# The last tile of targets walked in two passes of two row blocks each

## The chip, the cores and the metric

The kernel runs on one core of a Trainium2 chip. The metric is the device time of one execution in microseconds (us). Three runs of the kernel before took 810.81, 811.78 and 812.55 us; the median is 811.78 us. The profile is that of one more execution, which took 810.83 us.

## The reference, cut to what matters

Two graph layers over 4096 nodes with 128 features and a 4096 x 4096 integer adjacency matrix. The first takes, for each node, the maximum of its neighbours' features; the second is a graph attention layer. Only the second is touched by the change:

```python
h = jnp.maximum(_layernorm(x, axis=-1), 0.0)
x = x + _L0_gnn_ref(h, adj)                    # masked maximum over the neighbours
h = jnp.maximum(_layernorm(x, axis=-1), 0.0)
# _L1_gnn_ref(h, adj, W, a):
h = input @ W
e = (h @ a1)[:, None] + (h @ a2)[None, :]
e = jnp.where(e > 0, e, ALPHA * e)
e = jnp.where(adj > 0, e, NEG)
attention = jax.nn.softmax(e, axis=1)
h_prime = attention @ h
x = x + jax.nn.elu(h_prime)
```

## The kernel before, in words

The first 520 us or so make the masked maximum and also write the transposed adjacency, as 16-bit numbers, to `edge_units` in the chip's memory. The attention layer starts near 536 us. Its targets (the rows of the result) are cut into `TILES` = 8 tiles of `TI` = 512 targets, each of `ROWS` = 4 row blocks of 128. For each tile the kernel walks over `C` = 32 chunks of 128 sources. One pair (tile q, chunk c) is a step, and the list `ORDER` (line 166) gives the order of the steps: tiles 0 and 1 are walked in alternation, tiles 2 to 7 one after another, 32 steps each.

One step is this. VectorE (DVE) makes the unnormalised attention weights of 128 sources by 512 targets with a single instruction, `weigh(n)` (line 1016): the maximum of a row (`limit`) and a per-partition scalar (`slope`), times the adjacency. TensorE (PE) then does `mix(n)` (line 674): one float32 product for each of the four row blocks, with the weights loaded into the array and `wh` (128 features and a column of ones, so 129 columns) streamed past. Each float32 product is two records of the profile, so a step is eight. The sums of a tile stay in two PSUM banks (`out_ps`); even and odd tiles use different ones.

The two engines are tied by counting semaphores. `made` counts the weights that VectorE has made, `mixed` the steps that TensorE has done. There are `WEIGHTS` = 6 weight buffers, so VectorE may start step n only when step n-6 is done (line 1015). The adjacency comes in units of 8 steps of 1 MB each, four a tile, into `EDGES` = 4 buffers. SyncE (SP) loads a unit as soon as the last step that reads the unit before it in that buffer is made (line 289).

When a tile's last step is done, its output goes through these functions:

- `invert(q)` (line 1019) on VectorE copies the four columns of sums from PSUM (line 1023) and takes their reciprocal (line 1025). It stands in VectorE's program behind the weight of the fifth step of the next tile.
- `norm(q)` on ScalarE (ACT) scales the four row blocks from PSUM into `att` (line 477), and later takes an exponential (line 482).
- `cut(q)` on GpSimd (POOL), for tiles 0 to 6: two tensor-scalar instructions (lines 353 and 354), two tensor-tensor additions (lines 356 and 359), all 128 x 512, and the store (line 361).
- For tile 7, the last, the same arithmetic stands on VectorE (lines 1183 to 1189), behind four small instructions that test the size of the denominators (lines 1175 to 1179), and SyncE stores (line 293).

Behind that, a flag (`den_flag`, line 1191) is read by TensorE, ScalarE, VectorE and SyncE, which then branch over a part of the program that isn't run for these inputs. With that the kernel ends.

Of the kernel before, what the change touches and what calls it, by code (L numbers as in the profile page):

```python
# [79 lines left out]
def layers(nc, adj, x_rows, w, a, edge_units, subset_max, out_rows, w_sb, a12, w_in, hs, x1_in, h_hi, h_lo, ident_h, ident32, order_w, bit_w, word,  # L80
# [4 lines left out]
    with ctx:  # L85
# [80 lines left out]
        ORDER = [(q, c) for lo, hi in PARTS for q in range(2) for c in range(lo * ROWS, hi * ROWS)]  # L166
        ORDER += [(q, c) for q in range(2, TILES) for c in range(C)]
        PLACE = {at: n for n, at in enumerate(ORDER)}
        ENDS = [PLACE[q, C - 1] for q in range(TILES)]
        LOADED = list(dict.fromkeys(q * UNITS + c // (UNIT * PAIR) for q, c in ORDER))  # L170
# [4 lines left out]
        EDGES = 4  # L175
        WEIGHTS = 6
        ALL = TILES * C
# [59 lines left out]
        with nc.Block() as block:  # L237
            @block.sync
            def _(sp):
# [52 lines left out]
                sp.wait_ge(last_done, 1)  # L292
                sp.dma_start(out_rows[:, q * ROWS:(q + 1) * ROWS, :], low[:, q % 2, :, :]).then_inc(last_stored, 16)
                sp.wait_ge(last_stored, 16)
                sp.wait_ge(stored[0], 16 * (TILES // 2))
                sp.wait_ge(stored[1], 16 * (TILES // 2 - 1))

# [12 lines left out]
            def _(pool):  # L310
# [36 lines left out]

                def cut(q):
                    if q >= 2:
                        pool.wait_ge(stored[q % 2], 16 * (q // 2))  # L350
                    pool.wait_ge(normed, (q + 1) * ROWS)
                    al, ll = att[:, q % 2, :, :], low[:, q % 2, :, :]
                    nc.gpsimd.tensor_scalar(ll, al, 0.0, None, ALU.min).then_inc(low_made, 1)  # L353
                    nc.gpsimd.tensor_scalar(al, al, 0.0, -1.0, ALU.max, ALU.add).then_inc(kept_made, 1)
                    pool.wait_ge(kept_made, q + 1)
                    nc.gpsimd.tensor_tensor(al, al, x1[:, q * ROWS:(q + 1) * ROWS, :], ALU.add).then_inc(summed_up, 1)
                    pool.wait_ge(summed_up, q + 1)
                    pool.wait_ge(low_exp, q + 1)
                    nc.gpsimd.tensor_tensor(ll, ll, al, ALU.add).then_inc(finished, 1)
                    pool.wait_ge(finished, q + 1)  # L360
                    nc.gpsimd.dma_start(out_rows[:, q * ROWS:(q + 1) * ROWS, :], ll).then_inc(stored[q % 2], 16)

                for q in range(TILES - 1):
                    cut(q)

            @block.scalar
            def _(act):
# [102 lines left out]

                def norm(q):
                    act.wait_ge(rden_made, q + 1)
                    if q >= 2:
                        act.wait_ge(finished, q - 1)
                    for b in range(ROWS):
                        r = q * ROWS + b
                        nc.scalar.activation(att[:, q % 2, b, :], out_ps(q, b)[:, 0:D], ACT.Copy, scale=rden[:, r:r + 1]).then_inc(normed, 1)  # L477
                    if q == TILES - 1:
                        act.wait_ge(last_low, 1)
                    else:  # L480
                        act.wait_ge(low_made, q + 1)
                    nc.scalar.activation(low[:, q % 2, :, :], low[:, q % 2, :, :], ACT.Exp).then_inc(low_exp, 1)

# [34 lines left out]
                for q in range(2, TILES):  # L518
                    if q + 1 < TILES:
                        bound(q + 1)  # L520
                    norm(q)

                act.wait_ge(flag_made, 1)
# [14 lines left out]
            def _(pe):  # L538
# [122 lines left out]
                def mix(n):  # L661
                    q, c = ORDER[n]
                    pe.wait_ge(made, n + 1)
                    if q == 0:
                        pe.wait_ge(wh_made, c + 1)
                        if c % ROWS == 0:
                            pe.wait_ge(wh_last, c // ROWS + 1)
                    if c == 0:
                        if q == 1:
                            pe.wait_ge(joined, 6)  # L670
                        elif q >= 2:
                            pe.wait_ge(normed, (q - 1) * ROWS)
                    for b in range(ROWS):
                        last = nc.tensor.matmul(out_ps(q, b), weight[:, n % WEIGHTS, b * P:(b + 1) * P], wh[:, c, :],  # L674
                                                start=c == 0 and b % 2 == 0, stop=c == C - 1 and b % 2 == 1)
                    last.then_inc(mixed, 1)
# [140 lines left out]
            def _(dve):  # L817
# [201 lines left out]
                def invert(q):  # L1019
                    dve.wait_ge(mixed, ENDS[q] + 1)  # L1020
                    for b in range(ROWS):
                        r = q * ROWS + b
                        V.tensor_copy(den[:, r:r + 1], out_ps(q, b)[:, D:D + 1]).then_inc(den_made, 1)
                    dve.wait_ge(den_made, (q + 1) * ROWS)
                    V.reciprocal(rden[:, q * ROWS:(q + 1) * ROWS], den[:, q * ROWS:(q + 1) * ROWS]).then_inc(rden_made, 1)  # L1025

# [102 lines left out]
                for n in range(ALL):  # L1129
                    q, c = ORDER[n]  # L1130
                    if c == 0:
                        cap(q)
# [39 lines left out]
                al, ll = att[:, q % 2, :, :], low[:, q % 2, :, :]  # L1172
                dve.wait_ge(rden_made, TILES)
                dve.wait_ge(curves, GR)
# [10 lines left out]
                dve.wait_ge(last_sum, 1)  # L1185
                V.tensor_tensor(al, al, x1[:, q * ROWS:(q + 1) * ROWS, :], ALU.add).then_inc(last_sum, 1)
                dve.wait_ge(last_sum, 2)
                dve.wait_ge(low_exp, TILES)
                V.tensor_tensor(ll, ll, al, ALU.add).then_inc(last_done, 1)
# [61 lines left out]
```

## Time and profile before

| | |
|---|---|
| runs, lowest / median / highest | 810.81 / 811.78 / 812.55 us |
| profiled execution: time | 810.83 us |
| its span, first to last instruction | 809.0 us |
| TensorE busy | 709.9 us (88%) |
| VectorE busy | 720.6 us (89%) |
| ScalarE busy | 485.5 us (60%) |
| GpSimd busy | 282.8 us (35%) |

The time lies 1.9 us above the span: that is what lies around the instructions. "Busy" is the time in which an engine has an instruction in hand, and the records of neighbouring instructions may overlap, so the distance from one start to the next says more than a duration. All times in the rows are counted from the start of the span. The granted clock is the share of full speed (2.4 GHz) that TensorE was given.

### The profile page before, as it was taken

The page shows a single profiled execution, that of the slowest core. Times are in us where ns is not written, and L with a number is a line of the kernel's source. Part 1 is how long each engine was busy: PE and PEld are TensorE (multiplying, and loading weights), DVE is VectorE, ACT ScalarE, POOL GpSimd, SP SyncE. Part 2 cuts the span into 40 slices and gives each one's busy share as a digit, 9 for nine tenths or more (in the row PEclk, how much of TensorE's full clock was granted, in tenths as well). Part 3 has the DMA queues.
Part 4 walks back from the last instruction along what each step waited for, and adds up shares of the span by engine and source line. Part 5 has one row for each costly group of instructions (what it writes and reads, how often), then busy time and mean ns, then how long its engine had stood idle before and what let it go on. Part 6 is the DMA issues. An engine that isn't in the chain of part 4 may idle for free.

```text
span 809.0 us, 14805 instructions
## 1 busy us (share of the span) xinstructions
PE 709.9 (88%) x5594; PEld 488.4 (60%) x5594; DVE 720.6 (89%) x1116; ACT 485.5 (60%) x614; POOL 282.8 (35%) x258
## 2 busy tenths in 40 slices
PE   1788999999999999999999999476889999999995
PEld 1344444444444444444444445355889999999995
DVE  8899889999999999999999999886678998898994
ACT  2978888888888888888888886235423010010000
POOL 0611034434434435434444345354202531232130
PEclk9999999999999999999999999699899999999998
DMA  9799767997777867877787744523313544444410
GB/s 307 248 369 358 255 228 256 261 296 254 244 220 243 260 223 225 260 237 218 248 254 223 232 152 133 181 48 121 119 53 156 184 140 142 163 156 164 131 60 15
DMA packets 62857, 162.55 MB, mean 201 GB/s; under 512 B 6400, under 2 KB 11136, under 8 KB 58688
## 3 DMA queue, kind: packets, MB, share of 16 engines
q1 hardware_dynamic: 53776, 138.75, 49.5%
q0 software_dynamic: 9008, 22.82, 11.4%
q8 instruction: 47, 0.77, 0.4%
q14 instruction: 26, 0.21, 0.1%
HBM read 117.51 MB, written 44.04 MB: 200 GB/s over the span
## 4 chain that ended last, share of the span: by engine, by line
PE 45%; ACT 23%; DVE 17%; issue 11%; DMA 2%; POOL 1%; ACTq 0%; DVEq 0%; SPq 0%
PE pick_ps L674 27%; ACT edge_t L373 10%; DVE acc L850 7%; ACT depth L382 6%; PE order_ps L559 6%; PE pick_ps L578 6%; ACT first L381 4%; DVE rest L839 2%; PE late_ps L591 2%; PE late_ps L550 2%; DMA subset_max<-keys 1%; DVE rest L1016 1%; PE late_ps L658 1%; PE order_ps L643 1%; DVE acc L978 1%
## 5 line engine op out<-in xcount | busy, mean ns | idle before, releaser
L850 DVE TENSOR_TENSOR acc<-pick_ps,acc 128x1024 f32<-128x1024 f32 x248 | 302.9, 1221 | 27.9 <-PE pick_ps L578 23.7
L345 POOL DMA_INDIRECT found<-subset_max,entry x192 | 205.2, 1069 | 288.7 <-DVE entry L862 180.7
L674 PE MATMUL pick_ps<-keys,rest 128*128 128x129 f32 x2048 | 240.4, 279 | 13.3 <-DVE rest L1016 12.6
L674 PEld LDWEIGHTS pick_ps<-keys,rest 128*128 128x128 f32 x2048 | 236.6, 195 | 19.6 <-DVE rest L1016 17.6
L1016 DVE SCALAR_TENSOR_TENSOR rest<-depth,acc,stage 128x512 f32<-128x512 f32 x256 | 200.2, 812 | 28.2 <-PE pick_ps L674 9.4
L381 ACT ACTIVATE first<-order_ps,neg 128x1024 f16<-128x1024 f32 x128 | 142.5, 1113 | 61.3 <-PE order_ps L559 61.3
L382 ACT ACTIVATE depth<-order_ps,mid 128x1024 f16<-128x1024 f32 x128 | 141.6, 1107 | 0.0
L373 ACT ACTIVATE edge_t<-late_ps 128x1024 f16<-128x1024 uint16 x128 | 131.0, 1023 | 2.8 <-PE late_ps L550 2.8
L559 PE MATMUL order_ps<-edge_t,order_w 128*128 128x512 f16 x256 | 79.2, 392 | 36.9 <-ACT edge_t L373 29.7
L578 PE MATMUL pick_ps<-first,h_hi 128*128 128x512 f16 x256 | 97.6, 381 | 6.8 <-DVE acc L850 6.7
L550 PEld LDWEIGHTS late_ps<-ident_h,stage 128*128 128x128 f16 x1024 | 69.3, 99 | 48.8 <-DMA stage<-adj 13.1
L578 PE MATMUL pick_ps<-second,h_hi 128*128 128x512 f16 x256 | 97.4, 380 | 0.4 <-DVE acc L850 0.4
L578 PE MATMUL pick_ps<-first,h_lo 128*128 128x512 f16 x256 | 97.6, 381 | 0.0
L578 PE MATMUL pick_ps<-second,h_lo 128*128 128x512 f16 x256 | 97.2, 380 | 0.0
L550 PE MATMUL late_ps<-ident_h,stage 128*128 128x128 f16 x1024 | 80.3, 223 | 17.1 <-DMA stage<-adj 13.1
L477 ACT ACTIVATE keys<-pick_ps,acc 128x128 f32<-128x128 f32 x32 | 9.1, 368 | 129.4 <-DVE acc L1025 129.4
L591 PEld LDWEIGHTS late_ps<-bit_w,rest 128*128 128x128 f16 x1024 | 62.6, 98 | 29.4 <-issue 14.5
L591 PE MATMUL late_ps<-bit_w,rest 128*128 128x128 f16 x1024 | 78.6, 220 | 0.0
L559 PEld LDWEIGHTS order_ps<-edge_t,order_w 128*128 128x128 f16 x256 | 15.5, 98 | 97.0 <-ACT edge_t L373 91.1
L353 POOL TENSOR_SCALAR keys<-keys 128x512 f32<-128x512 f32 x7 | 13.1, 1878 | 148.0 <-ACT keys L477 148.0
L833 DVE TENSOR_SCALAR second<-depth 128x2048 f16<-128x2048 f16 x64 | 44.4, 693 | 0.0
L839 DVE TENSOR_SCALAR rest<-depth 128x2048 f16<-128x2048 f16 x64 | 43.8, 685 | 0.0
(140 smaller groups left out, 519.3 us busy)
## 6 DMA issues: line engine op xcount, KB each, us to landing
stage<-adj SPq DMA_DIRECT2D x64, 1024.0 KB, 5.4
edge_units<-edge_t SPq DMA_DIRECT2D x64, 512.0 KB, 4.4
stage<-edge_units SPq DMA_DIRECT2D x32, 1024.0 KB, 4.9
subset_max<-keys POOLq DMA_DIRECT2D x12, 512.0 KB, 8.7
found<-subset_max,entry POOLq DMA_INDIRECT x192, 4.3
best<-x SPq DMA_DIRECT2D x4, 512.0 KB, 6.1
subset_max<-x POOLq DMA_DIRECT2D x4, 512.0 KB, 8.9
out<-keys POOLq DMA_DIRECT2D x7, 256.0 KB, 2.8
```

Of the source, the lines that this page charges most:

```text
L345: nc.gpsimd.indirect_dma_start(found[:, n % NG, s, :], None, subset_max, bass.IndirectOffsetOnAxis(entry[:, n, s:s + 1], 0)).then_inc(gath ...
L373: nc.scalar.activation(edge_t[:, g % (KEPT * KEEP), :], flip_ps[:, :].bitcast(U16), ACT.Sign).then_inc(edge_ready, 1)
L381: nc.scalar.activation(first[:, g % 4, :], order_ps[:, :], ACT.Relu, scale=-1.0, bias=neg[:, :]).then_inc(first_ready, 1)
L382: nc.scalar.activation(depth[:, g % 4, :], order_ps[:, :], ACT.Abs, bias=mid[:, :]).then_inc(depth_ready, 1)
L550: last = nc.tensor.transpose(flip_ps[:, c * TI + r * P:c * TI + (r + 1) * P], low[:, (s * PAIR + c) * P:(s * PAIR + c + 1) * P], ident_h[: ...
L559: last = nc.tensor.matmul(order_ps[:, c * TI:(c + 1) * TI], order_w[:, :], edge_t[:, g % (KEPT * KEEP), c * TI:(c + 1) * TI], start=True, ...
L578: last = nc.tensor.matmul(pick_ps[k][:, c * TI:(c + 1) * TI], half_h[:, p * PAIR + c, :], s[:, c * TI:(c + 1) * TI], start=part == 0, stop ...
L591: last = nc.tensor.matmul(key_ps[:, r * P:(r + 1) * P], rest[:, g % RESTS, c * TI + r * P:c * TI + (r + 1) * P], bit_w[:, b, :], start=Fal ...
L674: last = nc.tensor.matmul(out_ps(q, b), weight[:, n % WEIGHTS, b * P:(b + 1) * P], wh[:, c, :], start=c == 0 and b % 2 == 0, stop=c == C - ...
L839: V.tensor_scalar(rest[:, to:to + 2, :], depth[:, at:at + 2, :], MID - 1.5, None, ALU.is_lt).then_inc(rest_ready, 1)
L850: V.tensor_tensor(acc[:, q % 2, :], pick_ps[k][:, :], acc[:, q % 2, :], ALU.max).then_inc(raised, 1)
L1016: V.scalar_tensor_tensor(out=weight[:, n % WEIGHTS, :], in0=limit[:, q % 2, :], scalar=slope[:, c:c + 1], in1=units[:, m % EDGES, k * TI:( ...
```

## The change

`ORDER` gets 32 further steps: tile 7 is now walked twice. `SEGS` lists nine segments (tile, first row block, last row block): tiles 0 to 6 whole, then row blocks 0 and 1 of tile 7, then row blocks 2 and 3. `span_of(n)` gives the row blocks of step n. In a step of the two last segments VectorE makes 256 columns of weights and TensorE does two products. `ENDS` has nine entries, one for each segment, and `invert`, `norm` and `cut` count segments instead of tiles. The first half of tile 7 now goes through GpSimd's `cut`, 256 columns wide, and GpSimd's store; VectorE's closing arithmetic and SyncE's store take only the second half. The units of adjacency are still loaded once each (`LOADED` drops repetitions), and all four units of tile 7 have a buffer of their own.

```diff
-        PLACE = {at: n for n, at in enumerate(ORDER)}
-        ENDS = [PLACE[q, C - 1] for q in range(TILES)]
+        ORDER += [(TILES - 1, c) for c in range(C)]
+        SEGS = [(q, 0, ROWS) for q in range(TILES - 1)] + [(TILES - 1, 0, ROWS // 2), (TILES - 1, ROWS // 2, ROWS)]
+        ENDS = [n for n, (q, c) in enumerate(ORDER) if c == C - 1]
+        span_of = lambda n: (0, ROWS) if n <= ENDS[TILES - 2] else SEGS[TILES - 1][1:] if n <= ENDS[TILES - 1] else SEGS[TILES][1:]
...
-                sp.dma_start(out_rows[:, q * ROWS:(q + 1) * ROWS, :], low[:, q % 2, :, :]).then_inc(last_stored, 16)
+                sp.dma_start(out_rows[:, q * ROWS + ROWS // 2:(q + 1) * ROWS, :], low[:, q % 2, ROWS // 2:ROWS, :]).then_inc(last_stored, 16)
...
-                for q in range(TILES - 1):
-                    cut(q)
+                for k in range(len(SEGS) - 1):
+                    cut(k)
...
-                    for b in range(ROWS):
+                    for b in range(lo, hi):
                         r = q * ROWS + b
                         nc.scalar.activation(att[:, q % 2, b, :], out_ps(q, b)[:, 0:D], ACT.Copy, scale=rden[:, r:r + 1]).then_inc(normed, 1)
...
-                    for b in range(ROWS):
+                    for b in range(*span_of(n)):
                         last = nc.tensor.matmul(out_ps(q, b), weight[:, n % WEIGHTS, b * P:(b + 1) * P], wh[:, c, :],
...
-                    V.scalar_tensor_tensor(out=weight[:, n % WEIGHTS, :], in0=limit[:, q % 2, :], scalar=slope[:, c:c + 1],
-                                           in1=units[:, m % EDGES, k * TI:(k + 1) * TI], op0=ALU.max, op1=ALU.mult).then_inc(made, 1)
+                    lo, hi = (b * P for b in span_of(n))
+                    V.scalar_tensor_tensor(out=weight[:, n % WEIGHTS, lo:hi], in0=limit[:, q % 2, lo:hi], scalar=slope[:, c:c + 1],
+                                           in1=units[:, m % EDGES, k * TI + lo:k * TI + hi], op0=ALU.max, op1=ALU.mult).then_inc(made, 1)
...
-                invert(TILES - 1)
+                invert(TILES)
...
-                al, ll = att[:, q % 2, :, :], low[:, q % 2, :, :]
-                dve.wait_ge(rden_made, TILES)
+                al, ll = att[:, q % 2, ROWS // 2:ROWS, :], low[:, q % 2, ROWS // 2:ROWS, :]
+                dve.wait_ge(rden_made, TILES + 1)
```

On VectorE, from the sixth step of tile 7 to the closing arithmetic (`rest` is the memory that the weights lie in, `acc` holds the sums and their reciprocals), before:

```order
L1023 COPY acc<-pick_ps 128x1 [waits mixed]
L1023 COPY acc<-pick_ps 128x1 x3
L1025 RECIPROCAL acc<-acc 128x4 [waits den_made]
L1016 SCALAR_TENSOR_TENSOR rest<-depth,acc,stage 128x512 [waits mixed] x3
L1016 SCALAR_TENSOR_TENSOR rest<-depth,acc,stage 128x512 [waits mixed,edge_in1]
L1016 SCALAR_TENSOR_TENSOR rest<-depth,acc,stage 128x512 [waits mixed] x7
L1016 SCALAR_TENSOR_TENSOR rest<-depth,acc,stage 128x512 [waits mixed,edge_in2]
L1016 SCALAR_TENSOR_TENSOR rest<-depth,acc,stage 128x512 [waits mixed] x7
L1016 SCALAR_TENSOR_TENSOR rest<-depth,acc,stage 128x512 [waits mixed,edge_in3]
L1016 SCALAR_TENSOR_TENSOR rest<-depth,acc,stage 128x512 [waits mixed] x7
L1023 COPY acc<-pick_ps 128x1 [waits mixed]
```

The end of the first pass and the start of the second on the same engine, after (line 1022 is `weigh`, lines 1030 and 1032 are `invert`):

```order
L1022 SCALAR_TENSOR_TENSOR rest<-depth,acc,stage 128x256 [waits mixed,edge_in3]
L1022 SCALAR_TENSOR_TENSOR rest<-depth,acc,stage 128x256 [waits mixed] x7
L1022 SCALAR_TENSOR_TENSOR rest<-depth,acc,stage 128x256 [waits mixed,edge_in0]
L1022 SCALAR_TENSOR_TENSOR rest<-depth,acc,stage 128x256 [waits mixed] x4
L1030 COPY acc<-pick_ps 128x1 [waits mixed]
L1030 COPY acc<-pick_ps 128x1
L1032 RECIPROCAL acc<-acc 128x2 [waits den_made]
L1022 SCALAR_TENSOR_TENSOR rest<-depth,acc,stage 128x256 [waits mixed] x3
L1022 SCALAR_TENSOR_TENSOR rest<-depth,acc,stage 128x256 [waits mixed,edge_in1]
```

Where 32 instructions of 512 columns stood for tile 7, there are now 64 of 256 columns, with a second pair of copies and a reciprocal between the passes, and the waits on `mixed` and on the units occur twice.

On GpSimd, the end of the program before:

```order
L353 TENSOR_SCALAR keys<-keys 128x512 [waits normed,stored0]
L354 TENSOR_SCALAR keys<-keys 128x512
L356 TENSOR_TENSOR keys<-keys,x 128x512 [waits kept_made]
L359 TENSOR_TENSOR keys<-keys 128x512 [waits low_exp,summed_up]
L361 DMA out<-keys 128x4x128 [waits finished]
```

And after (lines 356 to 364 are what 353 to 361 were):

```order
L364 DMA out<-keys 128x4x128 [waits finished]
L356 TENSOR_SCALAR keys<-keys 128x256 [waits normed,stored1]
L357 TENSOR_SCALAR keys<-keys 128x256
L359 TENSOR_TENSOR keys<-keys,x 128x256 [waits kept_made]
L362 TENSOR_TENSOR keys<-keys 128x256 [waits low_exp,summed_up]
L364 DMA out<-keys 128x2x128 [waits finished]
```

GpSimd has one more round, of half the width, behind that of tile 6.

## Rows read from the trace of the kernel before

**Rows 1.** The page: span, and busy time of each engine (section 1).

```profile
span 809.0 us, 14805 instructions
PE 709.9 (88%) x5594; PEld 488.4 (60%) x5594; DVE 720.6 (89%) x1116; ACT 485.5 (60%) x614; POOL 282.8 (35%) x258
```

**Rows 2.** Chain that ended last, tiles 6 and 7: start us, us, what.

```profile
721.37 28.59 PE pick_ps L674 x256
749.95 0.86 PE order_ps L643 x2
750.81 49.15 PE pick_ps L674 x440
```

**Rows 3.** Same chain, its last piece, behind the last product.

```profile
799.98 0.37 DVE acc L1023 x4
800.35 0.02 issue
800.37 0.19 DVE acc L1025
800.56 0.02 issue
800.59 1.15 ACT keys L477 x4
801.74 0.03 issue
801.76 0.05 DVEq L1182
801.81 0.05 issue
801.86 0.43 DVE keys L1183
802.29 0.35 DVE keys L1184
...
802.66 0.70 DVE keys L1186
...
803.38 0.69 DVE keys L1189
804.08 0.06 DVE den_flag L1191
```

**Rows 4.** Timeline around the start of tile 7: start us, us, instruction.

```profile
771.40 0.36 DVE L1023 COPY acc<-pick_ps 128x1 f32<-128x1 f32 x4
771.79 0.18 DVE L1025 RECIPROCAL acc<-acc 128x4 f32<-128x4 f32 x1
771.88 2.06 DVE L1016 SCALAR_TENSOR_TENSOR rest<-depth,acc,stage 128x512 f32<-128x512 f32 x3
772.00 1.14 ACT L477 ACTIVATE keys<-pick_ps,acc 128x128 f32<-128x128 f32 x4 [20.40 <-DVE acc L1025]
773.30 1.98 POOL L353 TENSOR_SCALAR keys<-keys 128x512 f32<-128x512 f32 x1 [21.10 <-ACT keys L477]
774.15 14.08 DVE L1016 SCALAR_TENSOR_TENSOR rest<-depth,acc,stage 128x512 f32<-128x512 f32 x16 [0.21 <-PE pick_ps L674]
775.26 2.25 POOL L354 TENSOR_SCALAR keys<-keys 128x512 f32<-128x512 f32 x1
777.59 1.27 POOL L356 TENSOR_TENSOR keys<-keys,x 128x512 f32<-128x512 f32 x1
778.94 1.59 POOL L359 TENSOR_TENSOR keys<-keys 128x512 f32<-128x512 f32 x1
```

**Rows 5.** Timeline of VectorE alone, short stretches of tile 7.

```profile
774.15 2.59 DVE L1016 SCALAR_TENSOR_TENSOR rest<-depth,acc,stage 128x512 f32<-128x512 f32 x3 [0.21 <-PE pick_ps L674]
...
777.65 1.76 DVE L1016 SCALAR_TENSOR_TENSOR rest<-depth,acc,stage 128x512 f32<-128x512 f32 x1
779.33 2.41 DVE L1016 SCALAR_TENSOR_TENSOR rest<-depth,acc,stage 128x512 f32<-128x512 f32 x2
783.65 0.74 DVE L1016 SCALAR_TENSOR_TENSOR rest<-depth,acc,stage 128x512 f32<-128x512 f32 x1
784.32 1.40 DVE L1016 SCALAR_TENSOR_TENSOR rest<-depth,acc,stage 128x512 f32<-128x512 f32 x2
```

**Rows 6.** The same engine in tile 2, working off a backlog, and GpSimd beside it.

```profile
629.99 2.56 DVE L1016 SCALAR_TENSOR_TENSOR rest<-depth,acc,stage 128x512 f32<-128x512 f32 x2
631.01 2.56 DVE L1016 SCALAR_TENSOR_TENSOR rest<-depth,acc,stage 128x512 f32<-128x512 f32 x2
632.47 1.76 DVE L1016 SCALAR_TENSOR_TENSOR rest<-depth,acc,stage 128x512 f32<-128x512 f32 x2
630.71 1.73 POOL L353 TENSOR_SCALAR keys<-keys 128x512 f32<-128x512 f32 x1
632.42 1.92 POOL L354 TENSOR_SCALAR keys<-keys 128x512 f32<-128x512 f32 x1
```

**Rows 7.** VectorE's instructions by form, whole span: busy us, mean ns of one.

```profile
L873 DVE TENSOR_TENSOR found<-found 128x384 f32<-128x384 f32 x32 | 17.6, 551 | 1.3 <-issue 1.3
L873 DVE TENSOR_TENSOR found<-found 128x128 f32<-128x128 f32 x32 | 9.1, 283 | 0.2
L1023 DVE COPY acc<-pick_ps 128x1 f32<-128x1 f32 x32 | 2.8, 150 | 5.3 <-PE pick_ps L674 4.6
```

**Rows 8.** TensorE's line 674 from 771.4 to 785.7: ns min/median/max.

```profile
L674 PE MATMUL pick_ps<-keys,rest x130: 273/276/276, 771.2 to 785.6; 128*128 128x129 f32 x130
```

**Rows 9.** Windows: PE, PEld, DVE, ACT, POOL busy, granted clock, DMA share, GB/s.

```profile
563.04:566.45 3.41, 0.72 (x6) 0.72 (x7) 2.55 (x9) 2.04 (x6) 1.80 (x2) 1.00 0.21 37
563.00:575.00 12.00, 9.27 (x68) 9.27 (x69) 10.75 (x22) 5.40 (x14) 6.63 (x6) 0.86 0.36 106
597.17:600.59 3.42, 2.14 (x20) 1.95 (x19) 2.33 (x5) 0.00 (x0) 0.00 (x0) 1.00 0.00 0
600.59:604.00 3.41, 2.48 (x21) 2.28 (x21) 3.19 (x13) 0.30 (x1) 0.00 (x0) 1.00 0.02 5
771.40:800.00 28.60, 28.55 (x256) 28.35 (x254) 22.00 (x33) 1.77 (x5) 7.89 (x5) 1.00 0.04 11
```

**Rows 10.** DMA issues of the whole run (page, section 6) and the last store's.

```profile
stage<-edge_units SPq DMA_DIRECT2D x32, 1024.0 KB, 4.9
...
out<-keys SPq DMA_DIRECT2D x1, 256.0 KB, 2.4
```

More of the change, by code:

```diff
@@ L176, in layers @@
         WEIGHTS = 6
-        ALL = TILES * C
+        ALL = len(ORDER)
         PER = UNIT * PAIR
@@ L292, in _ @@
                 sp.wait_ge(last_done, 1)
-                sp.dma_start(out_rows[:, q * ROWS:(q + 1) * ROWS, :], low[:, q % 2, :, :]).then_inc(last_stored, 16)
+                sp.dma_start(out_rows[:, q * ROWS + ROWS // 2:(q + 1) * ROWS, :], low[:, q % 2, ROWS // 2:ROWS, :]).then_inc(last_stored, 16)
                 sp.wait_ge(last_stored, 16)
                 sp.wait_ge(stored[0], 16 * (TILES // 2))
-                sp.wait_ge(stored[1], 16 * (TILES // 2 - 1))
+                sp.wait_ge(stored[1], 16 * (TILES // 2))
                 sp.wait_ge(flag_made, 1)
@@ L346, in _, with cut @@
                                                      bass.IndirectOffsetOnAxis(entry[:, n, s:s + 1], 0)).then_inc(gathered[n % NG][s % 2], 16)
-                def cut(q):
+                def cut(k):
+                    q, lo, hi = SEGS[k]
                     if q >= 2:
                         pool.wait_ge(stored[q % 2], 16 * (q // 2))
-                    pool.wait_ge(normed, (q + 1) * ROWS)
-                    al, ll = att[:, q % 2, :, :], low[:, q % 2, :, :]
+                    pool.wait_ge(normed, q * ROWS + hi)
+                    al, ll = att[:, q % 2, lo:hi, :], low[:, q % 2, lo:hi, :]
                     nc.gpsimd.tensor_scalar(ll, al, 0.0, None, ALU.min).then_inc(low_made, 1)
                     nc.gpsimd.tensor_scalar(al, al, 0.0, -1.0, ALU.max, ALU.add).then_inc(kept_made, 1)
[L355 to L358, printed above, removed]
+                    pool.wait_ge(kept_made, k + 1)
+                    nc.gpsimd.tensor_tensor(al, al, x1[:, q * ROWS + lo:q * ROWS + hi, :], ALU.add).then_inc(summed_up, 1)
+                    pool.wait_ge(summed_up, k + 1)
+                    pool.wait_ge(low_exp, k + 1)
                     nc.gpsimd.tensor_tensor(ll, ll, al, ALU.add).then_inc(finished, 1)
-                    pool.wait_ge(finished, q + 1)
-                    nc.gpsimd.dma_start(out_rows[:, q * ROWS:(q + 1) * ROWS, :], ll).then_inc(stored[q % 2], 16)
-                for q in range(TILES - 1):
-                    cut(q)
+                    pool.wait_ge(finished, k + 1)
+                    nc.gpsimd.dma_start(out_rows[:, q * ROWS + lo:q * ROWS + hi, :], ll).then_inc(stored[q % 2], 16)
+                for k in range(len(SEGS) - 1):
+                    cut(k)
             @block.scalar
@@ L469, in gather_wh, with norm @@
                         nc.scalar.activation(wh[:, c, 0:D], wh_of(g, c % ROWS), ACT.Copy, scale=gain[:, c:c + 1]).then_inc(wh_made, 1)
-                def norm(q):
-                    act.wait_ge(rden_made, q + 1)
+                def norm(k):
+                    q, lo, hi = SEGS[k]
+                    act.wait_ge(rden_made, k + 1)
                     if q >= 2:
                         act.wait_ge(finished, q - 1)
-                    for b in range(ROWS):
+                    for b in range(lo, hi):
                         r = q * ROWS + b
                         nc.scalar.activation(att[:, q % 2, b, :], out_ps(q, b)[:, 0:D], ACT.Copy, scale=rden[:, r:r + 1]).then_inc(normed, 1)
-                    if q == TILES - 1:
+                    if k == TILES:
                         act.wait_ge(last_low, 1)
                     else:
-                        act.wait_ge(low_made, q + 1)
-                    nc.scalar.activation(low[:, q % 2, :, :], low[:, q % 2, :, :], ACT.Exp).then_inc(low_exp, 1)
+                        act.wait_ge(low_made, k + 1)
+                    nc.scalar.activation(low[:, q % 2, lo:hi, :], low[:, q % 2, lo:hi, :], ACT.Exp).then_inc(low_exp, 1)
                 root(0)
@@ L521, in _ @@
                     norm(q)
+                norm(TILES)
                 act.wait_ge(flag_made, 1)
@@ L1015, in weigh, with invert @@
                         dve.wait_ge(mixed, n - WEIGHTS + 1)
-                    V.scalar_tensor_tensor(out=weight[:, n % WEIGHTS, :], in0=limit[:, q % 2, :], scalar=slope[:, c:c + 1],
-                                           in1=units[:, m % EDGES, k * TI:(k + 1) * TI], op0=ALU.max, op1=ALU.mult).then_inc(made, 1)
-                def invert(q):
-                    dve.wait_ge(mixed, ENDS[q] + 1)
-                    for b in range(ROWS):
+                    lo, hi = (b * P for b in span_of(n))
+                    V.scalar_tensor_tensor(out=weight[:, n % WEIGHTS, lo:hi], in0=limit[:, q % 2, lo:hi], scalar=slope[:, c:c + 1],
+                                           in1=units[:, m % EDGES, k * TI + lo:k * TI + hi], op0=ALU.max, op1=ALU.mult).then_inc(made, 1)
+                def invert(k):
+                    q, lo, hi = SEGS[k]
+                    dve.wait_ge(mixed, ENDS[k] + 1)
+                    for b in range(lo, hi):
                         r = q * ROWS + b
                         V.tensor_copy(den[:, r:r + 1], out_ps(q, b)[:, D:D + 1]).then_inc(den_made, 1)
-                    dve.wait_ge(den_made, (q + 1) * ROWS)
-                    V.reciprocal(rden[:, q * ROWS:(q + 1) * ROWS], den[:, q * ROWS:(q + 1) * ROWS]).then_inc(rden_made, 1)
+                    dve.wait_ge(den_made, q * ROWS + hi)
+                    V.reciprocal(rden[:, q * ROWS + lo:q * ROWS + hi], den[:, q * ROWS + lo:q * ROWS + hi]).then_inc(rden_made, 1)
                 dve.wait_ge(folded, LAST)
@@ L1130, in _ @@
                     q, c = ORDER[n]
-                    if c == 0:
+                    if c == 0 and n <= ENDS[TILES - 1]:
                         cap(q)
@@ L1168, in _ @@
                         invert(ENDS.index(n - WEIGHTS + 1))
-                invert(TILES - 1)
+                invert(TILES)
                 q = TILES - 1
-                al, ll = att[:, q % 2, :, :], low[:, q % 2, :, :]
-                dve.wait_ge(rden_made, TILES)
+                al, ll = att[:, q % 2, ROWS // 2:ROWS, :], low[:, q % 2, ROWS // 2:ROWS, :]
+                dve.wait_ge(rden_made, TILES + 1)
                 dve.wait_ge(curves, GR)
@@ L1185, in _ @@
                 dve.wait_ge(last_sum, 1)
-                V.tensor_tensor(al, al, x1[:, q * ROWS:(q + 1) * ROWS, :], ALU.add).then_inc(last_sum, 1)
+                V.tensor_tensor(al, al, x1[:, q * ROWS + ROWS // 2:(q + 1) * ROWS, :], ALU.add).then_inc(last_sum, 1)
                 dve.wait_ge(last_sum, 2)
-                dve.wait_ge(low_exp, TILES)
+                dve.wait_ge(low_exp, TILES + 1)
                 V.tensor_tensor(ll, ll, al, ALU.add).then_inc(last_done, 1)
```

## The prediction

> **What bounds the kernel now.** I read the page's first section, then the chain that ended last, then the same stretch in windows and timelines. Over the whole span TensorE and VectorE are both near 89% busy [rows 1], which doesn't say who waits. The chain does: a whole tile is one piece of TensorE's line 674, 256 records in 28.59 us, and the last piece before the end is again that line [rows 2]. So a step (8 records) costs 28.59 / 32 = 0.893 us, and in tile 7 TensorE has no gap worth naming: 28.55 us busy of 28.60, at the full clock of 2.4 GHz [rows 9]. Behind its last product comes a chain of VectorE and ScalarE from 799.98 to 804.14 us [rows 3], and then 4.8 us more (flag, branches, the store's landing) to the end of the span. The change works on that chain and pays in tile 7's steps.
>
> **What the change takes away: the tail.** Each link of [rows 3] is halved in width or number. Two of four copies go: the four take 0.37 and one 0.15 [rows 7], so they start 0.07 apart, and two fewer are 0.13 to 0.15; I take 0.13. Two of four scalings go: 1.15 / 4 = 0.29 each by busy time, but the last one's record outlasts the start distance; from 800.59 to 801.74 with a last record of about 0.37, the distance is 0.26, so 0.52. VectorE's four tests in between still fit beside them: they now end about when ScalarE does. Line 1183 to the start of line 1186 is 0.80 us now. At a slope of (551 - 283) / 256 = 1.05 ns a column [rows 7] a two-input instruction loses 0.27 us from 256 columns; these two one-input ones take 0.43 us for 512, so about half that each, together 0.26. Lines 1186 and 1189 lose 0.27 each, 0.54. The exponential (off the chain before) stays off it. Sum: 0.13 + 0.52 + 0.26 + 0.54 = 1.45 us. The store of 256 KB, 2.4 us to landing [rows 10], becomes 128 KB. It ends before TensorE's branch does, so it counts only if the fetch behind that branch waits for it: bounds 0 and 0.5, I take 0.2. Gain: 1.65 us.
>
> **What it costs on TensorE.** The number of products is the same, 1024 records' worth of work in 32 whole or 64 half steps, so a half step is 0.447 us. Products that start a step with a wait are no slower than others: of 130 consecutive records none is below 273 or above 276 ns [rows 8]. I count nothing for 32 more waits. No load is added: SyncE still issues 32 unit loads, and the last one is issued when tile 6's last weight is made, 24 half steps (10.7 us) before it is needed, against 4.9 us to landing [rows 10].
>
> **What it costs on VectorE: the cover gets thin.** A whole weight instruction takes 0.66 us from start to start when VectorE doesn't wait (783.65, 784.32: [rows 5]), against TensorE's 0.893. Of that 512 columns at 1.04 ns are 0.533, the rest, 0.13, is fixed. A half one should take 0.267 + 0.13 = 0.40 us, against 0.447. VectorE's reserve drops from 26% to 11%: it gains back only 0.05 us a step. This is the unmeasured number. Below, if part of the fixed time scaled too, it is 0.66 / 2 = 0.33; above, a 128-column two-input instruction takes 283 ns and a 384-column one 551 [rows 7], which makes 0.42 for 256, plus the 0.05 by which line 1016 (0.74) exceeds the same-width 0.69 of line 1189: 0.47 if nothing overlaps. I take 0.40, since neighbouring records do overlap by 0.08 (0.74 against 0.66) in this very line.
>
> How far may VectorE fall behind before TensorE stops? Six buffers: it starts step n+6 when step n ends, and TensorE needs it five steps later, less the 0.28 us by which a step's first weight load precedes the end of the last product. In whole steps that is 4.47 - 0.28 - 0.04 - 0.78 = 3.4 us; in half steps 2.23 - 0.28 - 0.04 - 0.48 = 1.43 us. What disturbs VectorE is the work of the tile before, and it is unchanged for tile 6:
>
> - `invert` of tile 6: 771.40 to 771.88 [rows 4], 0.49.
> - GpSimd's two additions. VectorE's weight instruction of 777.65 lasts 1.76 instead of 0.74, and the one after that starts at 779.33 and, with its successor, takes 2.41 instead of 1.40 [rows 4, 5]: 1.02 + 1.01 = 2.03 us lost. Before, 3.4 us of cover held this. Now 1.43 doesn't.
> - GpSimd's two tensor-scalar instructions. Bounds: at 774 to 777 nothing shows (three weight instructions in 2.59 us, the pace of TensorE: the loss lies in VectorE's idle time [rows 5]); with VectorE working without a break three of them, from 629.99 to about 633.5, take 3.5 us instead of 1.99, so 1.5 lost [rows 6]. In the changed kernel VectorE is catching up from `invert` just then, yet has short instructions. I take 1.0.
> - Two waits for units, 0.07 each (the start of 774.15, 0.07 later than the pace): 0.14.
>
> Sum 3.66 us by about 780.5. In the remaining 9.1 - 3.7 = 5.4 us VectorE does 13.6 half instructions and regains 13.6 x 0.05 = 0.7. TensorE stops for 3.66 - 1.43 - 0.7 = 1.5 us.
>
> The second disturbance is new: the first part's own `invert` (two copies, 0.36) and its `cut` at half width (tensor-scalars 0.5, additions 1.0 to 1.1), and three unit waits, 0.2: 2.1 us. The first pass ends near 771.1 + 14.3 + 1.5 = 786.9; scaling, four GpSimd instructions of half width, and it is over by about 792.4. Since 780.5 that leaves 11.9 - 2.1 = 9.8 us, 24.5 instructions, 1.2 us regained from a lead of nothing. Stop: 0.9 us. From 792.4 to the end GpSimd is silent, and TensorE sets the pace. Its store is out well before 800 us. Together 2.4 us.
>
> *A page beside the row.* The row says 0.13 us fixed. The Trainium skill, "VectorE: DVE Perf Modes", section on the TRN2 errata, says that SBUF latency is exposed between instructions, once each, and advises tiles of at least 512 elements; it gives about 150 cycles fixed, 0.156 us at 0.96 GHz. By the page (an estimate) a half instruction is 0.42 us, only 0.02 are regained a step, and the stops would sum to 3.5 us instead of 2.4. The rule speaks against this change; trace and page agree in kind, and differ by 0.03 us.
>
> **Sum.** Against the profiled execution's own 810.83 us: -1.65 + 2.4 = +0.75, 811.6 us. That execution lies 0.95 below the median of the runs, 811.78. What will be measured is a median, so I state the forecast there: 811.78 + 0.75, about 812.4 us.
>
> **Rivals.** What can be told from no change is 0.2%, 1.6 us either way (810.2 to 813.4).
>
> - *The cover holds* (0.16). If a half instruction takes 0.35 us or less and the tensor-scalars hide, the first account is 0.49 + 2.03 + 0.14 = 2.66, less 1.43 and (9.1 - 2.7) / 0.35 x 0.097 = 1.8: no stop, nor in the second. Then the gain stands whole: 811.78 - 1.65 = 810.1. For it: the quiet stretch at 774 to 777. Against it: the fixed time would have to shrink with the width.
> - *VectorE becomes the bound* (0.22). The point of decision is 0.447 us: if a half weight instruction, with its wait and its semaphore, takes more, each of 64 steps is late and no lead is ever regained. At 0.46: 64 x 0.013 = 0.8, disturbances with tensor-scalars at their upper bound 0.49 + 1.5 + 2.03 + 0.14 + 0.36 + 0.75 + 1.1 + 0.2 = 6.6, less 1.43: 6.0 us of stops, +4.3, 816.1. Milder forms of it (0.42, tensor-scalars 1.5) end at 813.5 to 814.5. For it: lone records of 283 and 551 ns. Against: the overlap of records in line 1016.
> - *GpSimd shuts VectorE out for all its instructions* (0.03). As a mechanism here: the tensor-scalars of 1.98 and 2.25 us would hold VectorE for about 4.2 us instead of 1.0, and those of the first part for 2.1 instead of 0.5: +4.8, 817. At 774 to 777 VectorE runs at full pace beside them [rows 4, 5], so this is as good as excluded. The Trainium skill, "SBUF — State Buffer", section "Who interferes with whom", says that a VectorE instruction with two SBUF inputs and a GpSimd one that reads SBUF exclude each other for the whole instruction. By that rule the trace agrees for the additions (1.76 us), and disagrees for the tensor-scalars.
> - *It doesn't do what it says* (in the forecast's chance): GpSimd's part for the first half would have to last beyond 800 us. It has 13 us for what takes 6.
>
> TensorE's clock is no rival: with 2.14 and 2.48 us busy of 3.41 (597 to 604) it stayed at 2.4 GHz, and fell after a stretch with 0.72 of 3.41 busy [rows 9]. Stops of 1.5 and 0.9 us leave it busier than the former.
>
> **Numbers.** Forecast (0.59): 812.4, its own range 811 to 813.6. The range of 80% reaches from most of the first rival's to the milder forms of the second: 810.4 to 814.6. Faster by over 0.2% needs the cover to hold nearly whole: 0.13. Slower by over 0.2% takes the second and third rivals but for their mildest forms: 0.20. Within: 0.67.
>
> **What the profile after would show.** Half weight instructions 0.40 us apart where VectorE is behind, right after 771.9 (over 0.447: second rival; 0.35: first). The two instructions under GpSimd's additions near 777.7 lasting about 1.5 us. TensorE idle with VectorE's line 1022 as the releaser, once near 779 to 781 for about 1.5 us and once near 790 to 792 for about 0.9; none after. From TensorE's last product to the flag 2.7 us instead of 4.2. I am wrong if those idle times are missing or exceed 4 us, or if TensorE's half steps aren't 0.447 us without waits.

## The result, and the profile after

Over 20 runs each, the changed kernel takes 810.29 us in the median (809.65 to 812.13) and the kernel before 811.85 (810.24 to 813.40). The medians differ by 1.56 us. The ratio of the two kernels' times, with its 95% interval, is 0.9983 (0.9976 to 0.9991): 1.4 us faster (0.7 to 1.9). Two further comparisons of the same pair gave 0.9999 (0.9990 to 1.0008) and 0.9991 (0.9981 to 1.0001); the mean of the three is 0.9991, 0.7 us faster. The forecast was 812.4 us with a range of 810.4 to 814.6: the direction was wrong, and the first result lies just below the range. It lies within the 0.2% either way to which the prediction gave 0.67.

The profiled execution after took 811.00 us, span 809.2. That is 0.2 more than the span of before, and yet the kernel is faster. The profile lets the parts be told apart. The copy behind tile 6's last product starts at 771.99 instead of 771.40 (0.59 later, in a part of the program that wasn't changed), and what follows is shorter by 0.35 us. The chain that ended last (start us, us, what) from there on:

```profile
771.96 0.02 issue
771.99 0.37 DVE acc L1030 x4
772.35 0.02 issue
772.37 0.18 DVE acc L1032
772.55 0.80 DVE rest L1022 x3
773.35 0.28 issue
773.63 3.29 DVE rest L1022 x7
776.92 0.19 issue
777.12 3.70 DVE rest L1022 x4
780.81 0.04 issue
780.86 20.95 PE pick_ps L679 x184
801.80 0.02 issue
801.83 0.23 DVE acc L1030 x2
```

In [rows 2] this stretch was one piece of TensorE. Now VectorE's weights (line 1022) carry the first 9 us of it, and the chain stays on TensorE from 780.86. From copy to copy it is 801.83 - 771.99 = 29.84 us, against 799.98 - 771.40 = 28.58 before, 1.26 us longer. (To the end of the last product, as the table below counts, it is 29.80 against 28.55: 1.25 us.) The start distances of TensorE's products put its stops at 779.3 to 781.1 (1.13 us) and at 793.5 to 793.7 (0.12, inside the chain's long piece from 780.86 on). The clock isn't part of it. For the same stretch, columns as in [rows 9]:

```profile
772.00:801.80 29.80, 29.10 (x256) 28.57 (x254) 28.09 (x67) 2.81 (x8) 11.97 (x10) 1.00 0.05 15
```

TensorE's granted clock was 1.00 (2.4 GHz) throughout, as before. The tail, same columns, answers to [rows 3]:

```profile
802.28 0.19 DVE acc L1182
802.47 0.10 DVE acc L1183
802.57 0.02 issue
802.60 0.17 DVE acc L1185
802.76 0.02 issue
802.78 0.16 DVE acc L1186
...
803.04 0.30 DVE keys L1190
803.34 0.21 DVE keys L1191
...
803.57 0.43 DVE keys L1193
804.01 0.02 issue
804.03 0.43 DVE keys L1196
804.46 0.06 DVE den_flag L1198
```

ScalarE's two scalings are no longer in the chain; VectorE's four tests beside them end 0.04 us later than they do (802.94 and 802.90). From the copy at 801.83 to the end of the flag it is 2.69 us, and 4.16 before: 1.47 us shorter.

The timeline of VectorE (start us, us, instruction) in the first pass, short stretches as in [rows 5], shows what 256 columns cost alone, beside GpSimd's tensor-scalars, and beside its additions:

```profile
784.29 0.87 DVE L1022 SCALAR_TENSOR_TENSOR rest<-depth,acc,stage 128x256 f32<-128x256 f32 x2
...
774.03 1.23 DVE L1022 SCALAR_TENSOR_TENSOR rest<-depth,acc,stage 128x256 f32<-128x256 f32 x2
775.58 1.22 DVE L1022 SCALAR_TENSOR_TENSOR rest<-depth,acc,stage 128x256 f32<-128x256 f32 x2
777.91 2.89 DVE L1022 SCALAR_TENSOR_TENSOR rest<-depth,acc,stage 128x256 f32<-128x256 f32 x2
```

A free pair takes 0.87: 0.396 to the next start and 0.471 for the record. The pair at 774.03 has lost 0.36 us, that at 775.58 has lost 0.35, and the pair at 777.91 has lost 2.02. And GpSimd beside it, answering to [rows 4], with the first part's round behind it:

```profile
773.89 1.57 POOL L356 TENSOR_SCALAR keys<-keys 128x512 f32<-128x512 f32 x1 [21.08 <-ACT keys L481]
775.44 2.00 POOL L357 TENSOR_SCALAR keys<-keys 128x512 f32<-128x512 f32 x1
...
777.53 1.59 POOL L359 TENSOR_TENSOR keys<-keys,x 128x512 f32<-128x512 f32 x1
779.19 1.32 POOL L362 TENSOR_TENSOR keys<-keys 128x512 f32<-128x512 f32 x1
...
789.09 1.05 POOL L356 TENSOR_SCALAR keys<-keys 128x256 f32<-128x256 f32 x1 [7.45 <-ACT keys L481]
790.12 1.17 POOL L357 TENSOR_SCALAR keys<-keys 128x256 f32<-128x256 f32 x1
...
791.38 0.90 POOL L359 TENSOR_TENSOR keys<-keys,x 128x256 f32<-128x256 f32 x1
792.35 0.79 POOL L362 TENSOR_TENSOR keys<-keys 128x256 f32<-128x256 f32 x1
```

The arithmetic of the first part is over at 793.1, 8.7 us before the last product. Its store is issued at 793.44 and lands 2.3 us later. So the closing work that the change moved lies beside products of TensorE, off the chain.

### The profile page after: what moved, and what is told of

Read it like the earlier page. It is cut to its first block, busy times and chain, and to the rows that moved or that the text cites. A ratio compares the mean times of both kernels' runs of the same rounds, so it can differ in the third digit from the quotient of the medians.

```text
span 809.2 us, 14852 instructions
## 1 busy us (share of the span) xinstructions
PE 710.1 (88%) x5594; PEld 487.5 (60%) x5594; DVE 724.5 (90%) x1149; ACT 485.8 (60%) x615; POOL 285.1 (35%) x263
## 4 chain that ended last, share of the span: by engine, by line
PE 44%; ACT 23%; DVE 18%; issue 11%; DMA 2%; POOL 1%; ACTq 0%; DVEq 0%; SPq 0%
PE pick_ps L679 26%; ACT edge_t L376 10%; DVE acc L855 7%; ACT depth L385 6%; PE order_ps L564 6%; PE pick_ps L583 6%; ACT first L384 4%; DVE rest L1022 2%; DVE rest L844 2%; PE late_ps L596 2%; PE late_ps L555 2%; DMA subset_max<-keys 1%; PE late_ps L663 1%; DVE acc L983 1%; PE order_ps L648 1%
## 5 line engine op out<-in xcount | busy, mean ns | idle before, releaser
L1022 DVE SCALAR_TENSOR_TENSOR rest<-depth,acc,stage 128x512 f32<-128x512 f32 (+1 forms) x288 | 204.9, 750 | 28.7 <-PE pick_ps L679 10.3
L356 POOL TENSOR_SCALAR keys<-keys 128x512 f32<-128x512 f32 (+1 forms) x8 | 13.8, 1723 | 156.7 <-ACT keys L481 156.7
```

What stands on the lines that cost most here:

```text
L1022: V.scalar_tensor_tensor(out=weight[:, n % WEIGHTS, lo:hi], in0=limit[:, q % 2, lo:hi], scalar=slope[:, c:c + 1], in1=units[:, m % EDGES, ...
```

## The experiments

VectorE's lead is the time for which TensorE can go on when VectorE stands still, from the weights already made. The theory after the result: the change costs stops of TensorE, each as long as VectorE is held up, less its lead and less what it regained; it gives back the shorter tail; nothing else moved. The sum of these pieces is called the local account. The main rival: something outside the last tile is faster by 1 us. Each ratio is to the kernel before, run on the same chips. The three last columns are times in us from one trace of each kernel, and the first of them starts at the copy behind tile 6's last product:

| kernel | ratio (95% interval) | tile 6's copy to the end of the last product | last product to flag | flag to end |
|---|---|---|---|---|
| before | | 28.55 | 4.18 | 4.84 |
| before, once more | 1.0001 (0.9991 to 1.0010) | 28.55 | 4.18 | 4.80 |
| changed | 0.9983 (0.9976 to 0.9991) | 29.80 | 2.72 | 4.70 |
| changed, second | 0.9999 (0.9990 to 1.0008) | 29.80 | 2.72 | 4.78 |
| changed, third | 0.9991 (0.9981 to 1.0001) | 29.80 | 2.72 | 4.46 |
| two passes, closing whole | 1.0016 (1.0007 to 1.0026) | 29.68 | 4.19 | 5.00 |
| whole steps, half closing | 0.9984 (0.9974 to 0.9994) | 28.55 | 2.72 | 4.49 |
| five buffers | 0.9999 (0.9990 to 1.0008) | 30.27 | 2.72 | 4.56 |
| few additions for tile 6 | 0.9976 (0.9965 to 0.9987) | 28.55 | 2.72 | 4.56 |
| twelve half buffers | 0.9975 (0.9961 to 0.9990) | 28.55 | 2.72 | 4.76 |
| twelve, second | 0.9980 (0.9971 to 0.9990) | 28.55 | 2.73 | 4.85 |
| passes of three and one | 0.9980 (0.9971 to 0.9988) | 29.78 | 2.00 | 4.40 |

**The changed kernel again.** No edit.

> The changed kernel once more, to see what of its gain is local. In its first profile the local account is: TensorE stops 1.1 us near 780 and 0.1 near 793.5, the tail from last product to flag is 1.47 us shorter, flag to end 0.15 shorter: net -0.4 us, while the medians of 20 runs differ by -1.6. Theory A (the account is complete, the rest is scatter of the part before tile 6 and of the runs): the stop is again 1.1 + 0.1 us, the tail 2.7 us from last product to flag, and against the kernel before it is 0.0 to 0.8 us faster. Theory B (something besides the last tile is faster by about 1 us): again 1.2 to 1.9 us faster, with the same stops and the same tail, and the gain shows before tile 6 or behind the flag.

Measured: 0.9999. The stops and the tail to the flag repeat to the hundredth; the stretch from the flag to the end doesn't (4.70 and 4.78). That fits theory A. And a third time:

> The changed kernel a third time, for what is left of its gain: -1.4 us (ratio 0.9983) and -0.1 us (0.9999) so far, while both profiles give the same local account: stops 1.23 and 1.24 us, last product to flag 1.46 us shorter. Theory A (local account, everything else scatter): -0.4 us, and the profile again shows stops of 1.24 us. Theory B (a further gain of 1 us outside of it): -1.4 us.

Measured: 0.9991. The three ratios agree with a gain of 0.4 to 0.5 us within their intervals or nearly (the first interval ends at 0.9991, a gain of 0.7). The same pair of kernels gave 1.4, 0.1 and 0.7 us, so a single comparison can't decide over half a microsecond; the pieces from the traces can.

The traces also speak on theory B. Each of tiles 3 to 6 takes 29.44 to 29.45 us in all twelve profiles, and so does tile 2 except with five buffers. The end of tile 1 comes anywhere from 623.5 to 625.7 us: 624.1 and 625.4 in the two profiles of the kernel before, 624.7, 625.0 and 625.1 in those of the changed one. So most of the scatter of single runs arises ahead of tile 2, and no gain of 1 us shows there.

**Only the passes.** Against the kernel before:

```diff
+        ORDER += [(TILES - 1, c) for c in range(C)]
+        FIRST, HALFWAY = TILES * C - C, TILES * C
+        span_of = lambda n: (0, ROWS) if n < FIRST else (0, ROWS // 2) if n < HALFWAY else (ROWS // 2, ROWS)
...
-                    for b in range(ROWS):
+                    for b in range(*span_of(n)):
```

> Tile 7 is walked in two passes, but its four row blocks are normalised, closed and stored together at the end, as before. Only the cost of half steps is left. Theory A: the stop near 780 us stays at 1.1 us (VectorE's lead of 1.4 us against 3.2 us of disturbance from tile 6), the one near 793 goes, the tail is that of before: 1.1 us slower than before. Theory B: about 0 to 0.2 us slower, as the other gain of 1 us comes along with the second pass. Rival C (VectorE's half steps cost nothing): no stop, 0.0 us.

Measured: 1.0016, 1.3 us slower (0.6 to 2.1), with a stop of 1.13 us at 778.6 to 780.4 and none later. Rival C has fallen: half steps aren't free. Its chain (start us, us, what):

```profile
776.47 3.70 DVE rest L1020 x4
...
780.21 20.83 PE pick_ps L677 x184
```

**Only the short tail.** Against the kernel before; row blocks 0 and 1 of tile 7 are summed but neither scaled nor stored, so that part of the output is left out:

```diff
+                    lo = ROWS // 2 if q == TILES - 1 else 0
...
-                    for b in range(ROWS):
+                    for b in range(lo, ROWS):
...
-                al, ll = att[:, q % 2, :, :], low[:, q % 2, :, :]
+                al, ll = att[:, q % 2, ROWS // 2:ROWS, :], low[:, q % 2, ROWS // 2:ROWS, :]
```

> Tile 7 in whole steps, as before; row blocks 0 and 1 of it are neither normalised nor stored (left out), and the closing is that of row blocks 2 and 3 alone. Only the shorter tail is left. Theory A: last product to flag 2.7 us instead of 4.2, no stop of TensorE: 1.5 to 1.7 us faster than before. Theory B: the same profile; the changed kernel is as fast as this one although it has a stop of 1.2 us. Rival C: the tail isn't what ends the kernel (the branch behind the flag is), then below 0.5 us faster.

Measured: 0.9984, 1.3 us faster (0.5 to 2.1), 1.46 us less to the flag, and no stop:

```profile
770.97 28.38 PE pick_ps L675 x254
```

The two halves of the change are 1.3 us of cost against 1.3 us of gain in run times, each to within 0.8 us, and 1.13 (and 0.12 for the second round) against 1.46 in the traces.

**More lead.** Against the changed kernel; in tile 7 a buffer holds two half steps, and the `invert` of tile 6 stands behind the tenth half step:

```diff
+        slot = lambda n: n % WEIGHTS if whole(n) else (HALVES + (n - HALVES) // 2) % WEIGHTS
+        at = lambda n: 0 if whole(n) else (n - HALVES) % 2 * (TI // 2)
+        needs = lambda n: n - WEIGHTS + 1 if whole(n) else HALVES + (n - HALVES) // 2 - WEIGHTS + 1 if n < HALVES + 2 * WEIGHTS else n - 2 * WEIGHTS + 1
...
-                        dve.wait_ge(mixed, n - WEIGHTS + 1)
+                        dve.wait_ge(mixed, needs(n))
```

> The changed kernel, with each half of a weight buffer used by a half step of its own: in tile 7 VectorE may be 12 half steps ahead instead of 6, and the invert of tile 6 comes after the tenth half step. Lead 11 x 0.447 - 0.28 - 0.04 - 0.48 = 4.1 us against 3.2 us of disturbance. Theory A: no stop in either pass, 1.2 us faster than the changed kernel, 1.6 (local account) faster than before. Rival: the stop isn't for want of lead (it comes from the additions whatever the buffers): still 1.1 us near 780.

> The twelve half buffers once more, since the first comparison has an interval of 0.9961 to 0.9990. Local account: no stop, tail 1.46 us shorter: 1.5 us faster than before, about 1.2 faster than the changed kernel on the same chip.

Measured: 0.9975 and 0.9980, 2.0 and 1.6 us faster than before. VectorE is held up just as long (the pair of weight instructions under the additions lasts 2.90 us, 2.89 in the changed kernel), but the chain (start us, us, what) of the second run has TensorE in one piece again:

```profile
764.89 35.52 PE pick_ps L685 x318
800.42 0.02 issue
800.44 0.24 DVE acc L1036 x2
```

Against the changed kernel on the same chips the medians are 2.1 and 1.1 us lower (809.47 and 811.60; 809.54 and 810.60), where the account gives 1.2.

**Less lead.** Against the changed kernel: `WEIGHTS = 5`.

> The changed kernel with five weight buffers instead of six: VectorE's lead in half steps is 0.447 us shorter, 0.93 us instead of 1.38. Theory A (a stop is the disturbance less the lead and less what was regained): the stop near 780 grows from 1.13 to 1.58 us and the one near 793 from 0.10 to 0.1 to 0.2 (there the lead was empty before the second disturbance, so what counts is what is regained since); nothing in whole steps, where the lead is 2.5 us: 0.5 us slower than the changed kernel. Rival (TensorE stops for as long as the additions hold VectorE, whatever the lead): unchanged.

Measured: in tile 7 the stops are 1.58 us (780.3 to 782.6) and 0.14, as the account says. Chain of this kernel, same columns:

```profile
779.02 3.30 DVE rest L1022 x3
782.33 0.04 issue
782.37 21.42 PE pick_ps L679 x188
```

The expectation "nothing in whole steps" was wrong. Tile 2 took 29.97 us instead of 29.44, with a stop of 0.53 us:

```profile
638.42 1.77 DVE rest L1022
...
640.23 16.79 PE pick_ps L679 x148
```

That is the tile in which VectorE works off a backlog beside GpSimd's rounds [rows 6]: there it is behind already when the additions come, and a lead shorter by one whole step (0.893 us) no longer covers them. The median on the same chip is 811.08 us, and 810.60 for the changed kernel: 0.5 us more, which is the right way but not clear of the scatter, so the stops carry this test and the run time doesn't.

**Without the additions.** Against the changed kernel, two lines of `cut`; for tile 6 GpSimd adds 16 of 512 columns and leaves out the others:

```diff
-                    nc.gpsimd.tensor_tensor(al, al, x1[:, q * ROWS + lo:q * ROWS + hi, :], ALU.add).then_inc(summed_up, 1)
+                    few = lambda t: t[:, 0:1, 0:16] if k == TILES - 2 else t
+                    nc.gpsimd.tensor_tensor(few(al), few(al), few(x1[:, q * ROWS + lo:q * ROWS + hi, :]), ALU.add).then_inc(summed_up, 1)
...
-                    nc.gpsimd.tensor_tensor(ll, ll, al, ALU.add).then_inc(finished, 1)
+                    nc.gpsimd.tensor_tensor(few(ll), few(ll), few(al), ALU.add).then_inc(finished, 1)
```

> The changed kernel, but GpSimd's two additions for tile 6 take 16 of its 512 columns (the other columns of that tile are left out, so its output isn't the reference's). Theory A (the stop near 780 is the additions' 2.0 us on top of invert's 0.5 and the tensor-scalars' 0.7, less a lead of 1.4): disturbance 1.2 us, below the lead, so no stop near 780; the lead is full at the second disturbance and there is none near 793 either: 1.2 us faster than the changed kernel. Rival (half steps leave VectorE too little in any case, the tensor-scalars and invert suffice): a stop of 0.5 to 1 us stays.

Measured: 0.9976, 2.0 us faster than before, and no stop at all. GpSimd's tensor-scalars and VectorE's `invert` are as in the changed kernel and fit in the lead; the two additions are what empties it. Of the chain one piece, then GpSimd's timeline (start us, us):

```profile
770.90 29.61 PE pick_ps L680 x265
...
773.85 1.57 POOL L356 TENSOR_SCALAR keys<-keys 128x512 f32<-128x512 f32 x1 [21.09 <-ACT keys L482]
775.40 2.00 POOL L357 TENSOR_SCALAR keys<-keys 128x512 f32<-128x512 f32 x1
777.48 0.54 POOL L360 TENSOR_TENSOR keys<-keys,x 128x16 f32<-128x16 f32 x1
778.09 0.32 POOL L363 TENSOR_TENSOR keys<-keys 128x16 f32<-128x16 f32 x1
```

**Three row blocks, then one.** Against the changed kernel; a second-pass buffer holds four steps, the sums of the last block get another PSUM bank, and two tests go ahead of the last `invert`:

```diff
-        SEGS = [(q, 0, ROWS) for q in range(TILES - 1)] + [(TILES - 1, 0, ROWS // 2), (TILES - 1, ROWS // 2, ROWS)]
+        SEGS = [(q, 0, ROWS) for q in range(TILES - 1)] + [(TILES - 1, 0, ROWS - 1), (TILES - 1, ROWS - 1, ROWS)]
...
+                    if n == NARROW + 11:
+                        invert(TILES - 1)
```

> Tile 7 in a pass of three row blocks and a pass of one (whose sums get a PSUM bank of their own); in the second pass a weight buffer holds four steps, so VectorE may be 23 steps of 0.22 us ahead; the two tests that need no denominator stand ahead of the last invert. First pass: steps of 0.67 us on TensorE, 0.53 on VectorE, lead 5 x 0.67 - 0.28 - 0.04 - 0.6 = 2.4 us, disturbance 3.2 less 1.4 regained: no stop. Second: VectorE's 0.26 us against 0.22 loses 1.3 us in 32 steps, disturbances 2.4, lead 4.5: no stop. Tail 1.9 us instead of 2.7. Theory A: about 0.8 us faster than the twelve half buffers, 2.5 us faster than before. Rival: the second pass is VectorE's (0.26 or more a step, GpSimd's round at three quarters of the width), TensorE stops for 1 to 2 us near the end, no faster than twelve.

Measured: 0.9980, no better than twelve. The tail is 0.72 us shorter, as expected, but TensorE stops for 1.2 us at 798.1 to 800.6, which is what the rival said. VectorE's step is 0.263 us against TensorE's 0.223, and the expected lead was wrong: the `invert` behind the twelfth step of the second pass waits for the first pass to end, so VectorE is 12 steps ahead, not 23, just before GpSimd's round. Timeline (start us, us, instruction):

```profile
792.65 0.29 DVE L1036 COPY acc<-pick_ps 128x1 f32<-128x1 f32 x3
...
797.18 0.99 POOL L364 TENSOR_TENSOR keys<-keys,x 128x384 f32<-128x384 f32 x1
798.25 0.99 POOL L367 TENSOR_TENSOR keys<-keys 128x384 f32<-128x384 f32 x1
...
799.45 1.54 PE L685 MATMUL pick_ps<-keys,rest 128*128 128x129 f32 x10 [0.57 <-DVE rest L1028]
```

**The kernel before, in the place of a changed one.**

> The kernel before, unchanged, in the place of a changed one. Every variant so far comes out 0.3 to 0.9 us lower against it than its own local account says (the changed kernel 0.7 on the mean of three comparisons where the account gives 0.4). Theory A (scatter of the comparisons): ratio 1.000 within 0.001, no stop, last product to flag 4.2 us. Rival (what is compared with the kernel before gains some 0.4 us by its place in the order of runs, or the kernel before has been unlucky): ratio near 0.9995.

Measured: 1.0001. No bias shows, though the interval (0.9991 to 1.0010) doesn't exclude one of 0.4 us. The medians of the kernel before itself went from 810.76 to 811.85 us over the comparisons.

## Why the prediction was wrong, point by point

- *The tail: 1.45 us.* Right: 1.47 in the chain, and 1.45 or 1.46 in every profile with a half closing. That two of four scalings give 0.52 and the rest 0.93 holds too, though VectorE's tests now share the place of the scalings.
- *The store: 0.2 us.* Flag to end is 4.80 to 5.00 us in three profiles with a store of 256 KB and 4.40 to 4.85 in nine with a smaller one; the means are 4.88 and 4.62. The difference fits the size, but the two groups touch, and no run shows that the store is its cause or that the fetch behind the branch waits for it.
- *Half steps on TensorE: 0.447 us, waits for nothing.* Right: 28.55 us for 64 half steps wherever the lead suffices.
- *A half weight instruction: 0.40 us.* Right: 0.396, eighteen in a row from 780.7 on with records of 471 to 472 ns. By the 0.156 us of fixed time of the Trainium skill ("VectorE: DVE Perf Modes", the section on the TRN2 errata) it would have been 0.42; the trace has 0.396 - 0.267 = 0.13 of fixed time. The rival built on more than 0.447 has fallen, and so has that of 0.35.
- *The lead: 1.43 us.* Right within 0.05. The measured pieces of the first disturbance are 0.485 (`invert`), 0.71 (tensor-scalars), 2.02 (additions): 3.22. The stop was 1.13 and (780.72 - 771.99 - 3.22) / 0.396 x 0.051 = 0.71 were regained, so the lead was 3.22 - 0.71 - 1.13 = 1.38. That is a remainder, so the test is another kernel: with five buffers the stop grew by 0.45, one half step of 0.447.
- *The disturbances: 3.66 and 2.1 us.* This is the step that failed. In "GpSimd's two tensor-scalar instructions ... I take 1.0", the value was 0.71, between the bounds 0 and 1.5. (Why the same two instructions cost 1.5 us in tile 2 [rows 6] no run shows.) "Two waits for units, 0.07 each" was wrong: the wait is its own small instruction, but behind a busy VectorE it is done before the next start, and the distance stays 0.396. The row at 774.15 on which I had based it showed a VectorE that had been idle. So the first disturbance was 3.22 us. In the second I had 0.36 + 0.5 + 1.05 + 0.2 = 2.1; it was 0.325 + 0.28 + 0.95 = 1.55. The mechanism was right, and these two terms of the sum were too large.
- *The stops: 1.5 and 0.9 us.* They were 1.13 and 0.12, the second near 793.7 and not at 790 to 792. The second account shows how the error grew: 1.55 us of disturbance and 11.1 us in which 1.43 were regained leave 0.12, mine was 2.1 less 1.2. The stop is a small difference of two numbers of like size, and half a microsecond too much in the one became a stop seven times too long.
- *The sum: +0.75 us.* With the measured sizes: -1.46 - 0.26 + 1.25 = -0.5 us. The sum lay 1.2 us too high, of which the stops are 1.15. This error alone turned the direction, but it would have left the time, 811.78 - 0.5 = 811.3, inside the range. That the first result fell below 810.4 is best put down to the scatter of one comparison: it gave -1.4, the mean of three -0.7. (A slip besides: 811.78 + 0.75 is 812.53, not 812.4.)
- *GpSimd shuts VectorE out.* By the section "Who interferes with whom" of the Trainium skill, "SBUF — State Buffer", the two engines exclude each other for the whole instruction. For additions the trace agrees: the weight instruction lasts 1.49 and 1.48 us instead of 0.47. For the tensor-scalars, VectorE loses 0.36 of 1.57 us and 0.35 of 2.00: it is not shut out for their whole length.

What stays open: between the account (-0.5) and the mean of the comparisons (-0.7) lies less than one interval. No run shows a gain outside the last tile, but one of a few tenths of a microsecond ahead of tile 2 would be lost in the scatter there.

## What to carry to other kernels

Splitting the last tile shortens the tail by what is halved in it, but it also halves the lead in time that a fixed number of buffers gives the producing engine, so count the buffers in microseconds against the longest hold-up of that engine in the first pass. Here two half steps in each buffer turned a gain of 0.7 us (the mean of three comparisons) into one of 1.6 to 2.0. Where the cost is the difference of a disturbance and a cover, carry both bounds of each small term into the difference, since the errors of all of them land in it whole.

## What was not expected of the hardware

- A wait for a semaphore that has long been reached costs VectorE nothing while it has work in hand: 0.396 us to the next start with it and without it, in the stretch from 780.7 to 787.5 of the changed kernel. Behind an idle VectorE it cost 0.07 us [rows 4].
- GpSimd's tensor-scalars lasted 1.98 and 2.25 us beside whole weight instructions [rows 4] and 1.57 and 2.00 beside half ones. VectorE lost no start beside the former and 0.36 and 0.35 us beside the latter.
- An addition of 512 columns on GpSimd takes 1.01 us from VectorE's next weight instruction, whether that has 512 columns (1.76 instead of 0.74) or 256 (1.49 instead of 0.47); one of 256 columns takes 0.47.
